# Four graph layers on one core: a row buffer of the pruning pass becomes a fourth product buffer, and thresholds are computed earlier

## What is computed

```python
xn = x_comp / nrm[:, None]
cos = xn @ xn.T
edge_scores = softmax(cos * H / TAU, axis=1)
edge_mask = (edge_scores >= th_edge) & comp_mask[:, None]
H_pruned = H * edge_mask
connectivity = H_pruned.sum(axis=1)
...
agg = (H_pruned.T * dv_isqrt[None, :] @ transformed) * de_inv[:, None]
msg = (dv_isqrt[:, None] * (H_pruned @ agg)) @ Theta
```

## Time and profile before

| | us |
|---|---|
| median of 3 runs | 2391.56 |
| lowest and highest run | 2390.45, 2393.32 |
| the profiled execution | 2393.9 |
| its span (first to last instruction) | 2392.1 |
| TensorE busy | 2070.8 (87%) |
| VectorE busy | 1735.0 (73%) |
| ScalarE busy | 753.9 (32%) |
| moved by DMA | 828.91 MB, mean 347 GB/s |

### The profile page before, as it was taken

How to read it: one execution, slowest core, us unless ns; L and a number is a source line. 1 busy time by engine, 2 the same in 40 slices (tenths; PEclk the granted TensorE clock), 3 DMA queues, 4 the chain that set the end, 5 groups by cost and what they waited for, 6 DMA issues and landing times. The chain is left out here.

```text
span 2392.1 us, 36030 instructions
## 1 busy us (share of the span) xinstructions
PE 2070.8 (87%) x15658; PEld 736.6 (31%) x15658; DVE 1735.0 (73%) x2056; ACT 753.9 (32%) x869; POOL 4.5 (0%) x18
## 2 busy tenths in 40 slices
PE   7899998899976777799999989987777789997997
PEld 2224333222221111244444323221111134434333
DVE  5996743188889999955541358869999975555998
ACT  0001000066633333211110036643333311112897
POOL 0000000000000000000000000000000000000000
PEclk9999999999988888799999999988888899998999
DMA  9988999899559999977779989919999987775894
GB/s 374 421 352 364 421 428 428 362 404 372 225 240 401 414 387 417 390 267 269 276 301 396 427 365 381 378 74 394 386 412 393 412 323 281 283 283 229 337 420 176
DMA packets 130220, 828.91 MB, mean 347 GB/s; under 512 B 8464, under 2 KB 10512, under 8 KB 76560
## 3 DMA queue, kind: packets, MB, share of 16 engines
q1 hardware_dynamic: 128016, 825.29, 85.9%
q10 hardware_dynamic: 2048, 1.35, 0.2%
HBM read 690.29 MB, written 136.31 MB: 346 GB/s over the span
## 5 line engine op out<-in xcount | busy, mean ns | idle before, releaser
L1183 ACT ACTIVATE stream<-stream,negmax 128x4096 f32<-128x4096 f32 x128 | 475.2, 3713 | 514.0 <-DVE negmax L1177 514.0
L1136 PE MATMUL ps<-edgeT,node_twice 64*128 64x512 f32 x1024 | 284.5, 676 | 172.8 <-DVE mx L1172 172.7
L1172 DVE CUSTOM_DVE_ANT_0 stream<-ps,stream 128x1024 f32<-128x1024 f32 x296 | 347.8, 1220 | 41.5 <-PE ps L1136 27.2
L1136 PE MATMUL ps<-edgeT,query_twice 64*128 64x512 f32 x1024 | 249.5, 619 | 6.0 <-DVE edgeT L1379 3.7
L577 PE MATMUL ps<-stream,moved_block 128*64 128x512 f32 x960 | 216.3, 600 | 25.5 <-DMA stream<-in_adj 25.5
L1650 PE MATMUL ps<-stream,xw 32*64 32x512 f32 x4096 | 229.6, 589 | 2.6 <-issue 2.0
L1136 PEld LDWEIGHTS ps<-edgeT,node_twice 64*128 64x128 f32 x1024 | 95.2, 203 | 366.6 <-DVE mx L1172 260.6
L1154 PE MATMUL ps<-stream,ones 128*1 128x512 f32 x1024 | 187.0, 869 | 9.4 <-DVE stream L1691 9.4
L1217 ACT ACTIVATE query_twice<-ps,less_one_exponent 128x512 int32<-128x512 int32 x256 | 154.9, 687 | 14.4 <-PE ps L1307 12.1
L1691 DVE SCALAR_TENSOR_TENSOR stream<-stream,cut 128x4096 f32<-128x4096 f32 x34 | 152.5, 4485 | 1.2
L1754 DVE STREAM_TRANSPOSE stream<-spare 128x4096 f32<-128x4096 f32 x22 | 97.5, 4432 | 73.8 <-PE ps L1650 52.9
(11 more groups left out here) (233 smaller groups left out, 1954.2 us busy)
## 6 DMA issues: line engine op xcount, KB each, us to landing
stream<-in_adj SPq DMA_DIRECT2D x122, 2048.0 KB, 15.3
stream<-in_adjT SPq DMA_DIRECT2D x69, 2048.0 KB, 15.1
pruned<-stream SPq DMA_DIRECT2D x64, 2048.0 KB, 10.5
spare<-pruned SPq DMA_DIRECT2D x22, 2048.0 KB, 11.5
query_twice<-pruned SPq DMA_DIRECT2D x22, 2048.0 KB, 11.3
spare<-in_adj SPq DMA_DIRECT2D x20, 2048.0 KB, 10.0
moved_block<-in_adj SPq DMA_DIRECT2D x20, 2048.0 KB, 11.0
node_twice<-pruned SPq DMA_DIRECT2D x20, 2048.0 KB, 11.5
```

The lines of the kernel that those rows point to most:

```text
L1136: last = nc.tensor.matmul(ps[:, 2 * slot + h, :], stationary[F * h:F * h + F, rows_n], bank_of(edgeT[F * h:F * h + F, :], c), start=True, ...
L1172: nc.vector.tensor_tensor_reduce(out=prod[s][:, cols], in0=ps[:, 2 * slot:2 * slot + 2, :].rearrange("p a b -> p (a b)"), in1=block_in[:, ...
L1183: nc.scalar.activation(prod[s], prod[s], ACT.Exp, bias=negmax[:, s:s + 1], accum_out=zsum[:, s:s + 1]).then_inc(exp_done, 1)
```

## The change

- Row buffers: `places` keeps its six entries, but block n's place is no longer n % 6 throughout. From block 9 on five places are used and from block 24 on four (`place_of`). `held[2]`, a slot of `stream`, has block 3 as its last row block and is the fourth product buffer from block 5 on.
- Product buffers: `product_of` gives blocks 0 to 4 the three old ones and block 5 the new one, then all four in turn. Scoring waits for store and column sums of the last block in the same buffer. The small arrays `mx4`, `negmax`, `zsum` and `cut` get a fourth column, chosen by n % 4.
- Loads: m = n + 6 up to m = 8, n + 5 for 9 to 23, n + 4 from 24 on (`load_behind`), so no load follows stores 3 and 19.
- Thresholds: line 1686 leaves `prune` for a function of its own, called between the third and fourth chunk of the next block's score; for the last block just ahead of its masked product.
- Block 5 waits for the masked product of block 3, and turning chunk 2 for the last store from the new buffer.
- ScalarE's 32 calls are written out, where a loop ran over the last 21.

```diff
@@ -133,11 +133,11 @@
         per_partition = sb("per_partition", [P, 6])
         gl = {n: per_partition[:, i:i + 1]
               for i, n in enumerate(("gmax", "gmaxall", "gneg", "gsum", "gsumall", "grec"))}
-        mx4 = sb("mx4", [P, 3, 4])
-        negmax = sb("negmax", [P, 3])
-        zsum = sb("zsum", [P, 3])
-        rz = sb("rz", [P, 3])
-        cut = sb("cut", [P, 3])
+        mx4 = sb("mx4", [P, 4, 4])
+        negmax = sb("negmax", [P, 4])
+        zsum = sb("zsum", [P, 4])
+        rz = sb("rz", [P, 4])
+        cut = sb("cut", [P, 4])
         both_w = sb("both_w", [P, P])
         inverse = sb("inverse", [P, NB, 4])
         aggT = [curT[:, BANK * s:BANK * s + BANK] for s in range(2)]
@@ -1155,13 +1155,12 @@
                                             start=False, stop=False, skip_group_check=True)
             return last
-        def weighted_scores(dve, t, block_in, seen, scores_ready, chunk_used, max_ready, between=None):
-            s = t.k % SL3
+        def weighted_scores(dve, t, block_in, out, s, seen, scores_ready, chunk_used, max_ready, between=None):
             for c in range(NC):
                 slot = (NC * t.k + c) % SL3
                 if between and c == NC - 1:
@@ -1170,17 +1169,16 @@
                 dve.sem_inc(seen, 1)
                 cols = slice(CHUNK * c, CHUNK * c + CHUNK)
                 nc.vector.tensor_tensor_reduce(
-                    out=prod[s][:, cols], in0=ps[:, 2 * slot:2 * slot + 2, :].rearrange("p a b -> p (a b)"),
+                    out=out[:, cols], in0=ps[:, 2 * slot:2 * slot + 2, :].rearrange("p a b -> p (a b)"),
                     in1=block_in[:, cols], scale=1.0, scalar=NEG_HUGE, op0=ALU.mult, op1=ALU.max,
                     accum_out=mx4[:, s, c:c + 1]).then_inc(chunk_used, 1)
             dve.wait_ge(chunk_used, t.n * NC + NC)
             nc.vector.tensor_reduce(negmax[:, s:s + 1], mx4[:, s, :], AX.X, ALU.max, negate=True)\
                 .then_inc(max_ready, 1)
-        def exponentials(act, t, max_ready, exp_done):
-            s = t.k % SL3
+        def exponentials(act, t, out, s, max_ready, exp_done):
             act.wait_ge(max_ready, t.n + 1)
-            nc.scalar.activation(prod[s], prod[s], ACT.Exp, bias=negmax[:, s:s + 1],
+            nc.scalar.activation(out, out, ACT.Exp, bias=negmax[:, s:s + 1],
                                  accum_out=zsum[:, s:s + 1]).then_inc(exp_done, 1)
         def last_layer(block, sem, next_ahead, norm, msg_taken):
@@ -1420,7 +1418,8 @@
                         if t.k >= R:
                             dve.wait_ge(loaded[t.k % HELD], 16 * (t.turn(HELD, R) + 1))
                         wait(dve, summed, t.n - 2)
-                        weighted_scores(dve, t, held[t.k % HELD], seen, scores_ready, chunk_used, max_ready,
+                        weighted_scores(dve, t, held[t.k % HELD], prod[t.k % SL3], t.k % SL3, seen, scores_ready,
+                                        chunk_used, max_ready,
                                         (lambda: reciprocal(t.back(1))) if t.k >= 1 else None)
                     for n in range(NB):
                         body(last_step(n, seq))
@@ -1428,7 +1427,9 @@
                 @block.scalar
                 def _(act):
-                    row_blocks(act, 3, LEAD, lambda t: exponentials(act, t, max_ready, exp_done), seq)
+                    def body(t):
+                        exponentials(act, t, prod[t.k % SL3], t.k % SL3, max_ready, exp_done)
+                    row_blocks(act, 3, LEAD, body, seq)
@@ -1483,17 +1484,37 @@
                         v.tensor_tensor(bank_of(edgeT, k), bank_of(fold4b, k), bank_of(accT, k), ALU.mult)\
                             .then_inc(masked, 1)
-                HELD = 6
                 places = [held[0], held[1], held[4], held[2], held[3], q2[:, :]]
-                loaded = [sem(f"block_loaded{s}") for s in range(HELD)]
-                stored = [sem(f"block_stored{s}") for s in range(SL3)]
+                loaded = [sem(f"block_loaded{s}") for s in range(6)]
+                product = [*prod, held[2]]
+                stored = [sem(f"block_stored{s}") for s in range(4)]
                 scores_ready, chunk_used, max_ready = sem("scores_ready"), sem("chunk_used"), sem("max_ready")
                 seen = sem("scores_seen")
                 exp_done, cut_ready, pruned = sem("exp_done"), sem("cut_ready"), sem("pruned")
                 seq = [24, 25, 23, 21, 22, *range(26, NB), *range(21)]
-                R, LEAD = 5, 11
+                R = 5
+                def place_of(m):
+                    return m % 6 if m < 9 else (4, 5, 0, 1, 2)[(m - 9) % 5] if m < 24 else (5, 0, 1, 2)[m % 4]
+                def loads_before(m):
+                    return len([k for k in range(R, m) if place_of(k) == place_of(m)])
+                def product_of(n):
+                    return n % 3 if n < 5 else (3, 2, 0, 1)[(n - 5) % 4]
+                def stores_before(n, s):
+                    return len([k for k in range(n) if product_of(k) == s])
+                def load_behind(m):
+                    return m - 6 if m < 9 else m - 5 if m < 24 else m - 4
                 summed, rows_ready, deg_ready, inverse_ready, copies_ready, copies_taken = (
                     sem(n) for n in ("block_summed", "edge_sums_taken", "edge_sums_ready", "edge_inverse_ready",
@@ -1520,7 +1541,7 @@
                     return (n + 8) % NB
                 def buffer(t):
-                    return places[t.k % HELD]
+                    return places[place_of(t.n)]
                 @block.sync
                 def _(sp):
@@ -1532,18 +1553,18 @@
                             .then_inc(chunk_loaded[x % 3], 16)
                     def wait_stored(blocks):
-                        for s in range(SL3):
-                            sp.wait_ge(stored[s], 16 * len(range(s, blocks, SL3)))
+                        for s in range(4):
+                            sp.wait_ge(stored[s], 16 * stores_before(blocks, s))
                     def load(n):
-                        sp.dma_start(places[n % HELD], adj_b[seq[n]]).then_inc(loaded[n % HELD], 16)
+                        sp.dma_start(places[place_of(n)], adj_b[seq[n]]).then_inc(loaded[place_of(n)], 16)
                     load(R)
                     for n in range(NB):
                         sp.wait_ge(pruned, n + 1)
-                        sp.dma_start(Hp[seq[n]], prod[n % SL3]).then_inc(stored[n % SL3], 16)
+                        sp.dma_start(Hp[seq[n]], product[product_of(n)]).then_inc(stored[product_of(n)], 16)
                         for m in range(R + 1, NB):
-                            if n == m - HELD + (m >= 14) + (m >= 22):
+                            if n == load_behind(m):
                                 load(m)
                         if n == 28:
                             wait_stored(11)
@@ -1589,7 +1610,7 @@
                     def column_sum(t):
                         pe.wait_ge(pruned, t.n + 1)
-                        add_column_sums(ones[:, :], prod[t.k % SL3]).then_inc(summed, 1)
+                        add_column_sums(ones[:, :], product[product_of(t.n)]).then_inc(summed, 1)
                     def body(t):
                         score_products(pe, t, scores_ready, chunk_used, x2,
@@ -1680,36 +1701,46 @@
                 @block.vector
                 def _(dve):
-                    def prune(t):
-                        s = t.k % SL3
+                    def threshold(t):
+                        s = t.n % 4
                         dve.wait_ge(exp_done, t.n + 1)
                         nc.vector.scalar_tensor_tensor(
                             out=cut[:, s:s + 1], in0=zsum[:, s:s + 1], scalar=th,
                             in1=st["refuse"][:, bass.ds(t.block, 1)], op0=ALU.mult, op1=ALU.add)\
                             .then_inc(cut_ready, 1)
+                    def prune(t):
+                        s, kept = t.n % 4, product[product_of(t.n)]
                         dve.wait_ge(cut_ready, t.n + 1)
                         nc.vector.scalar_tensor_tensor(
-                            out=prod[s], in0=prod[s], scalar=cut[:, s:s + 1], in1=buffer(t),
+                            out=kept, in0=kept, scalar=cut[:, s:s + 1], in1=buffer(t),
                             op0=ALU.is_ge, op1=ALU.mult,
                             accum_out=st["conn"][:, bass.ds(t.block, 1)]).then_inc(pruned, 1)
                     def body(t):
-                        s = t.k % SL3
-                        if t.k >= R:
-                            dve.wait_ge(loaded[t.k % HELD], 16 * (t.turn(HELD, R) + 1))
-                        wait(dve, stored[s], t.turn(SL3) * 16)
-                        wait(dve, summed, t.n - 2)
-                        weighted_scores(dve, t, buffer(t), seen, scores_ready, chunk_used, max_ready)
-                        if t.k >= 1:
+                        s = product_of(t.n)
+                        if t.n >= R:
```

(16 more changed lines are left out.)

## The result

The changed kernel takes 2369.05 us (median of 4 runs, 2365.93 to 2370.71) against 2391.66: a ratio of 0.9897, 95% interval 0.9884 to 0.991, 22.6 us faster. Run again later, it took 2367.25 us against 2392.01 (0.9901, 0.9884 to 0.9917). The forecast was 2384.0 us with a range from 2379 to 2391: the direction was right, the size three times too small, and the range missed the time. The rival "much faster" had named 2369.1 us, with a chance of 0.07.

What follows compares the result with a forecast made beforehand. The prediction took the pruning pass to be bound by its DMA queue. Per pass, 3.7 (covered hole) + 0.4 (moved hole) - 0.4 (later first store) + 0.1 (shorter blocks) = 3.8; two passes 7.6, so 2391.56 - 7.6 = 2384.0 us, range 2379 to 2391.

Steps and rivals of the forecast that it cites:

- much faster: Rival, chance 0.07: the never-thin queue moves a pruning-pass transfer in 4.90 us (428 GB/s), 14.9 us more gain, 2369.1 us.
- What bounds the kernel: Pruning pass: first store to chunk 3's landing takes 62 DMA transfers plus the queue's idle time.
- what a transfer takes: Pruning pass: a 2048 KB transfer stays at 5.02 us, 418 GB/s; nothing given for it in the sum.
- The other term, idle time: Pruning pass: the DMA queue runs dry in two holes, mean 3.7 us each, where a block has no load.
- the covered hole: Block 19, which has no load: queue 9.0 us deep against 7.0 needed, so the hole closes, gaining 3.7 us a pass.
- little or nothing: Rival, chance 0.18: block 3's hole costs more and block 19's is only partly covered; 2388.4 us, or 2392.4 with nothing left.
- The hole moved to block 3: The hole moved from block 8 is paid again in a shallow queue, but shorter: 0.4 us gain, between 0 and 0.8.
- The threshold: Moved into the next block's score: first store 0.4 us later each pass, later VectorE blocks 0.1 us shorter.
- Late loads: From about block 23, VectorE waits for row buffers instead of stores, queue some 8 us deep; cost taken as 0.
- The tail: End of pass: TensorE idles longer before chunk 2, whose gather may slow; loss between 0 and 1.3 us, taken as 0.
- Slower through a deep queue: Rival, chance 0.10: more open transfers make each longer, 404 GB/s and 5.19 us; 2405.1 us.
- The signs: Forecast falls if block 19's hole stays, full stretches move under 413 GB/s, or chunk 3 waits for TensorE's earlier gathers.

Runs made afterwards that it cites:

- e3: The changed kernel with one wait more: scoring block n waits for the store of block n-3, as before the change; 2393.43 us.
- e5: The changed kernel with block n's wait for the store of block n-3 put ahead of the third chunk of its score; 2375.67 us.
- e2: The changed kernel with the threshold put back between the maximum and the masked product; four product buffers and new places kept; 2367.05 us.
- e4: The kernel before with only the new rhythm of loads, none behind stores 3 and 19; three product buffers, old thresholds; 2393.03 us.
- e1: The kernel before with only the threshold moved into the next block's score; three product buffers, six row buffers; 2391.98 us.
- e7: The changed kernel with 26 idle bf16 matmuls behind the gather of chunk 1 in each aggregation; 2366.24 us.
- e10: The kernel before with each load and store of the pruning passes split by columns into two DMAs of 1024 KB; 2396.34 us.

## Why the prediction was wrong

**What bounds the kernel: right.** The time from the first store to chunk 3 is 62 transfers plus idle time; e3 and e5 move it with nothing but a wait for a store.

**The term that failed is the one set to zero: what a transfer takes.** The prediction listed it as the third thing that can move the time, took 5.02 us from the 418 GB/s rows, and kept it, because the DMA share there was 1.00. But a share of 1.00 did not say that the queue gave all it could. The DMA queue's packets, megabytes and share of 16 engines, first of e3 from 1700 to 1760, then of the change from 1724 to 1764:

```profile
q1 hardware_dynamic: 1712, 24.92, 100.4%
```

```profile
q1 hardware_dynamic: 1175, 17.14, 100.4%
```

That is 1.004 x 16 x 60 / 1712 = 0.563 us a packet against 1.004 x 16 x 40 / 1175 = 0.547. The shallow queue's cost lies inside the packets and not in gaps. It is not spread evenly over them. Of the 16 KB packets of these two stretches, taken one by one from the traces, the middle one takes 611 ns in both; but 87 of e3's 1523 took over 700 ns, 982 on average, and only 6 of the change's 1047. 66 of the 87 start within 1 us of the landing of a row load, where the next store takes over. In the full stretch a transfer went from 5.02 to 4.89 us (429 GB/s); over both whole passes the packets took 9.2 us less than before, and 11.7 less than in e3.

**The other term, idle time, was right in kind and half the size.** The prediction took 3.7 for the covered hole and 0.4 for the moved one, 8.2 us in both passes; the traces lost 16.0. In the second pass the two holes idled 3.5 and 3.8 before and the one that is left 1.6, 5.7 of some 8; the rest are small dips, in the tail above all (share 0.99 before, 1.02 after). These two terms, packets 9.2 above the forecast and idle time 7.8 above it, more than make up the 15.0 us by which the median was missed; some 2 us come back elsewhere, among them the slow gathers below.

**The rival "much faster" hit its number partly by luck.** It stood at 0.07 and named 2369.1 us, from 14.9 us in the packets and the forecast's 7.6. Measured were 9.2 in the packets and 16.0 in idle time: the direction of its mechanism was right, its size too large, and the idle time made up for it. Against it stood that the 418 was seen in both long stretches; yet both were taken at the same depth, 3.3 us, so they could not say what a deeper queue would do. The rule of the Trainium skill that was weighed there (Perfetto Trace Analysis, Engine Utilization: about 435 GB/s for a core alone) gave the right direction; the runs end at 430.

**The covered hole: right.** Forecast were 3.7 us a pass. In e3 the window behind store 19 has a share of 0.67, so 3.3 idle; in the change it has 1.01. The depth at block 19 was 11.5 us (its store lands after 18.7), against the 9.0 forecast, so the margin that fed "little or nothing" was wider than it seemed: VectorE's block was 9.25 us and not 9.44, and from 7.2 at block 4 the landings grew by 1.7 a block to 12.2 at block 7, and by 0.5 later. In e2, with a block of 9.40, the depth there was 8.8 and covered the hole as well.

**The hole moved to block 3: no gain.** The prediction gave it 0.4 us of 0 to 0.8; the trace shows 1.6 us idle where an old hole had 3.7, and e4 shows that the place is worth nothing in time: what its idle time spares, its packets cost (2.9 less and 3.7 more in both passes). Why was not isolated.

**The threshold: right.** VectorE at the first iteration's first chunk and first masked product, in the change and in e2:

```profile
672.49 1.23 DVE L1171 CUSTOM_DVE_ANT_0 stream<-ps,stream 128x1024 f32<-128x1024 f32 x1 [0.88 <-PE ps L1136]
...
682.72 4.47 DVE L1715 SCALAR_TENSOR_TENSOR stream<-stream,cut 128x4096 f32<-128x4096 f32 x1
```

```profile
672.58 1.23 DVE L1171 CUSTOM_DVE_ANT_0 stream<-ps,stream 128x1024 f32<-128x1024 f32 x1 [0.55 <-PE ps L1136]
...
682.41 4.49 DVE L1716 SCALAR_TENSOR_TENSOR stream<-stream,cut 128x4096 f32<-128x4096 f32 x1
```

10.23 against 9.83 us: 0.40 later, as forecast. VectorE's block gets 0.14 shorter (9.40 to 9.26 between stores), where 0.1 was forecast. e1 and e2 show that it changes the time by less than can be measured.

**Late loads: right.** VectorE waits for rows from block 23 on, 0.4 us a block where 0.6 was forecast, with a queue 7.5 us deep, at 428 GB/s, and nothing is lost.

**The tail: taken at zero, was 1.1 us in the pass shown.** The bound was 1.3. The reason for zero, that a pause alone doesn't stand before a slow gather, was wrong: here it did, and e7 removed it.

**Slower through a deep queue: the opposite happened.** Its evidence, the 390 GB/s of the tail, was not a price of depth. The prediction's own reason against it holds: the chunk loads there have packets of 2 KB, whose middle one takes 84 ns in both kernels, 24.4 GB/s an engine against the 26.8 of a 16 KB packet in 611 ns.

**The signs.** Of the three that were to bring the forecast down, one came: the gather of chunk 3 waited for TensorE's own gather, 1.1 us. None of them looked at stretches faster than 418 GB/s, which is where the forecast broke.

## What to carry to other kernels

A pass that stands on its DMA queue can gain from one buffer more without a byte less. Read the depth of the queue as the landing time less that of a lone transfer; here it paid in the rate up to some 5 to 7 us, with transfers of 2 MB. That 5.0 us is also what one transfer takes is no rule: in e10 a transfer took half of that, more than one was queued (a half store landed after 7.0 us where a lone one takes 3.9), and the rate stayed at 416. A DMA share of 1.00 does not show that the rate is the best one: take the rate at two depths before it is called the ceiling. Beyond that, depth pays only as a cover for the places where a transfer is missing.

## What the runs showed of the hardware

- The rate of alternating stores and loads of 2 MB hangs on the time queued: 416 GB/s at 3.4 us, 425 at 4.0, 430 at 5.0, 430 at up to 12.8. The middle packet takes 611 ns in e3 as in the change; in e3 87 of 1523 take over 700 ns. Why is open; that more open DMAs alone cure it is ruled out by e10.
- DMAs of 64 partitions by 16 KB moved 321 GB/s in a pass where those of 128 partitions by 8 KB moved 416. It was seen in one run and not followed up.
- TensorE's granted clock was down behind a pause of 6.5 us. In the change it was 0.50 (third number from the end), the lower of its two levels (1.2 and 2.4 GHz), as the gather of chunk 2 began, which took 6.45 us. In e7, with bf16 matmuls on zeros in most of the pause, it was 1.00 from 1910 to 1917, and the same gather took 3.65, 2.80 less. The change, then e7:

```profile
1912.40:1914.00 1.60, 1.57 (x4) 0.59 (x6) 1.60 (x1) 0.00 (x0) 0.00 (x0) 0.50 1.05 397
```

```profile
1910.00:1917.00 7.00, 5.90 (x27) 2.46 (x26) 1.81 (x1) 0.00 (x0) 0.00 (x0) 1.00 0.92 337
```
